# Moving the second half of a broadcast burst behind a score matmul in a one-core attention and feed-forward kernel

## What is computed

```
sc = scores.reshape(b, h, nb, WIN, nb, WIN)          # WIN = 128, nb = 8
sc = jnp.where(causal, sc, NEG_INF)
m = jnp.max(sc, axis=-1, keepdims=True)
e = jnp.where(causal, jnp.exp(sc - m), 0.0)
probs = e / jnp.where(denom == 0.0, 1.0, denom)       # denom = jnp.sum(e, axis=-1)
...
attn_probs = jax.nn.softmax(probs, axis=-1)
attn_out = jnp.einsum('bhqk,bhkd->bhqd', attn_probs, v)
```

## Time and profile before

| what | value |
|---|---|
| median of 3 runs | 2334.8 us (2330.03 to 2336.23) |
| the profiled execution | 2336.34 us, its span 2334.5 us |
| PE busy | 2192.1 us, 94% |
| DVE busy | 1732.6 us, 74% |
| ACT busy | 1510.2 us, 65% |
| POOL busy | 1166.3 us, 50% |
| mean granted TensorE clock | 0.989 of full |

### The profile page before, as it was taken

The page is one execution under the profiler, slowest core; times in us unless marked ns, Lnnn a source line. Parts: engine busy times, 40 slices in busy tenths (PEclk is TensorE's granted clock), DMA queues, the critical chain, the costliest instruction groups (busy, mean ns, idle before and its releaser), DMA issues.

```text
span 2334.5 us, 47167 instructions
## 1 busy us (share of the span) xinstructions
PE 2192.1 (94%) x19388; PEld 1241.9 (53%) x19388; DVE 1732.6 (74%) x2115; ACT 1510.2 (65%) x2101; POOL 1166.3 (50%) x1126
## 2 busy tenths in 40 slices
PE   6889889999999999999999999999999999989998
PEld 4444344465555555455554555545555555545567
DVE  6787888767787676876778776776877767787466
ACT  2477676766666667676776666766666666667741
POOL 3144134545665456744676257763576544443540
PEclk8999999999999999999999999999999999999999
DMA  5233122211122113111133202231022211101000
GB/s 181 72 107 98 49 55 82 85 48 39 50 68 85 53 35 91 60 51 53 35 91 96 59 9 59 67 109 49 14 65 78 84 35 46 40 16 31 6 28 25
DMA packets 114067, 140.26 MB, mean 60 GB/s; under 512 B 8648, under 2 KB 86760, under 8 KB 113856
## 3 DMA queue, kind: packets, MB, share of 16 engines
q1 hardware_dynamic: 113856, 137.24, 20.7%
HBM read 74.28 MB, written 58.74 MB: 57 GB/s over the span
## 4 chain that ended last, share of the span: by engine, by line
PE 77%; DVE 15%; ACT 3%; DMA 2%; issue 2%; POOL 2%; SPq 1%; ACTq 0%; POOLq 0%
PE pv L822 11%; PE sums L812 9%; PE ring L772 9%; PE score L742 9%; PE score L797 9%; PE sums L754 9%; DVE e L1178 6%; PE score L691 5%; DVE negmax L1156 4%; PE ring L851 4%; PE score L706 3%; PE ring L775 2%; PE score L800 2%; PE score L682 2%; ACT e L1052 2%
## 5 line engine op out<-in xcount | busy, mean ns | idle before, releaser
L1052 ACT ACTIVATE e<-score 128x512 f32<-128x512 f32 x1152 | 670.9, 595 | 400.7 <-PE score L800 220.6
L1178 DVE TENSOR_TENSOR e<-ring,e 128x1024 f32<-128x1024 f32 x576 | 677.5, 1217 | 282.6 <-PE ring L851 281.9
L1156 DVE TENSOR_REDUCE negmax<-ring 128x8 f32<-128x1024 f32 x576 | 679.5, 1220 | 140.5 <-PE ring L775 133.9
L1057 ACT ACTIVATE e<-e 128x2048 f32<-128x2048 f32 x288 | 548.6, 1905 | 3.7 <-DVE e L1178 3.6
L797 PE MATMUL score<-q_st,k_st 112*128 112x512 bf16 (+3 forms) x1536 | 459.7, 331 | 39.2 <-ACT e L1052 22.0
L772 PE MATMUL ring<-k_st,q_st 96*128 96x512 bf16 (+3 forms) x1664 | 389.1, 319 | 53.7 <-DVE e L1178 25.1
L1493 POOL TENSOR_SCALAR r_p<-r_b,ab 128x256 bf16<-128x256 f32 x96 | 88.6, 923 | 531.8 <-DVE r_b L1184 531.8
L822 PE MATMUL pv<-e,v 128*17 128x512 f32 (+3 forms) x3072 | 314.1, 496 | 1.1 <-DVE o_t L1196 1.1
L812 PE MATMUL sums<-e,d_ones 128*32 128x256 f32 x4608 | 304.6, 382 | 1.3
L1472 POOL TENSOR_TENSOR gT<-gT 128x512 f32<-128x512 f32 x112 | 115.9, 1040 | 333.5 <-ACT gT L1025 333.5
L797 PEld LDWEIGHTS score<-q_st,k_st 112*128 112x128 bf16 x1536 | 147.8, 97 | 228.9 <-issue 118.6
(11 more groups left out here) (149 smaller groups left out, 2518.3 us busy)
## 6 DMA issues: line engine op xcount, KB each, us to landing
q_st<-q_parts SPq DMA_DIRECT2D x31, 768.0 KB, 5.9
k_st<-k_parts SPq DMA_DIRECT2D x31, 768.0 KB, 8.6
q_parts<-qk_p SPq DMA_DIRECT2D x30, 384.0 KB, 2.6
k_parts<-qk_p SPq DMA_DIRECT2D x28, 384.0 KB, 2.5
x_in<-in_x SPq DMA_DIRECT2D x8, 1024.0 KB, 5.6
q_parts<-qk_p SPq DMA_DIRECT2D x30, 256.0 KB, 2.9
x_res<-in_x SPq DMA_DIRECT2D x30, 256.0 KB, 4.4
k_parts<-qk_p SPq DMA_DIRECT2D x28, 256.0 KB, 2.9
```

The lines of the kernel that those rows point to most:

```text
L1052: act.activation(e[:, n % ES, hh, :], score[SCORE_SLOT["st", n, hh][0]][:, :], ACT.Exp, scale=DK ** -0.5).then_inc(e1_done, 1)
L1057: act.activation(v, v, ACT.Exp).then_inc(e2_done, 1)
L1156: dve.tensor_reduce(negmax[:, at:at + NB // heads, hh:hh + heads].rearrange("p w h -> p h w"), slot[:, :].rearrange("p (h a n) -> p h a n" ...
L1178: dve.tensor_tensor(v, ring[no % 2][:, :].rearrange("p (i n) -> p i n", i=2), v, ALU.mult).then_inc(ring_free, 1)
```

## The change

The call for the second pair of heads moves from directly behind that for the first pair to directly behind the step's first score. Nothing is added or removed, and no other engine's order changes.

```
                 if 0 <= n - LAG_R < NUNIT:
                     one_over_sums(n - LAG_R, 0)
-                    one_over_sums(n - LAG_R, 1)
                 if piece_first(n) and p[0]:
...
                     if n < NUNIT:
                         scores(n, hh)
+                    if hh == 0 and 0 <= n - LAG_R < NUNIT:
+                        one_over_sums(n - LAG_R, 1)
                     if hh == 3 and 2 in at:
```

## The result

The changed kernel takes 2408.5 us (median of 4 runs, 2406.4 to 2412.7) against 2333.5 us for the kernel before (4 runs). The ratio is 1.0325, with a 95% interval of 1.0311 to 1.034: 75 us, 3.2% slower. The forecast was 2402 us, in a range of 2360 to 2447.

What follows compares the result with a forecast made beforehand. PE was taken to bound the kernel. 110 us of added PE work less 46 hidden gave 64, a second count 72; 67 was taken, giving 2402 us against the median of 2334.8, range 2360 to 2447.

Steps and rivals of the forecast that it cites:

- What bounds it: Whole kernel: PE bounds it, busy 94% of the span and 77% of the chain, against 15% for DVE.
- No gain at the ring: Pair 1's wait for the slot DVE's last reduce still reads: gain about 0, upper bound 31.8 us.
- The price of a half: Pair 1 alone behind score 0 costs PE 0.39 us per step, 110 us over 283 steps.
- some hundred us: Sum over all steps by the rule alone that a change of tiling mode drains TensorE, two more per step.
- What is hidden: PE's waits for DVE's multiply, a reduce and ACT absorb 46 us of the 110, between 24 and 68.
- Pair 1 late in the ninth steps: DVE stands 0.7 us in each of 31 ninth steps; costed at nothing, 22 us without cover.
- Pair 1 in time elsewhere: Ordinary steps: pair 1 ready at 1.19 us, before DVE finishes pair 0 at 1.62 us, so not late.
- Nothing is hidden: Rival: waits move behind PE's added work; 110 us, or 132 with ninth-step lateness, 2445 to 2467 us; chance 0.15.
- most is hidden: Rival: entry to the strips costs 0 and all waits absorb; 17 us slower, 2352 us; chance 0.09.
- faster: Rival: score 0 fills a real 31.8 us stall at the weight loads, half is free; 2309 us; chance 0.03.
- no difference: Rival: the half behind the score runs inside the whole-array matmul's stream; 6 us; chance 0.03.
- The check on ACT: Sign to look for after the change: ACT waits some 60 us more for scores.

Runs made afterwards that it cites:

- not_ninth: The move made in all steps but the ninth ones (252 steps), against the kernel before: 2404.4 us, ratio 1.0310.
- full_between: The kernel before with one extra 128-column matmul on the whole array between the two pairs, nothing moved: 2428.8 us, ratio 1.0417.
- pair1_twice: The kernel before with the four matmuls of pair 1 issued twice in a row: 2365.1 us, ratio 1.0151.
- strip_between: The kernel before with one extra 128-column matmul on one strip of 32 rows between the two pairs, nothing moved: 2338.7 us, ratio 1.0034.

## Why the prediction was right

- **What bounds it.** PE, as it said. The chain went to 84% PE.
- **No gain at the ring.** Right: the 31.8 us on the weight loads were no stall. The burst's matmuls had 0.3 us of idle time before and 0.0 after, and the loads' wait for the reduce stayed (29.8 us in 72). The reading of that row was off, though: 75 of the 76 waits stand at the burst's first load, which is pair 0's, while PE still works on the key sums. It says next to nothing of pair 1. Score 0 gained what was said, 0.01 to 0.02 us.
- **The price of a half, 0.32 + 0.09 - 0.02 = 0.39 us.** Right for the parts that were named: 0.32 to 0.33, and 0.15 against 0.06 at the entry. Some 57 us of the 110 are the two changes of mode (0.09 + 0.11, 283 times), and the rest is lost overlap; so the forecast's "some hundred us" from the rule on such changes alone doesn't hold. One term was missing, too. Where a piece with 4-byte operands stands behind the half, its first matmul costs 0.05 to 0.1 us more: that of line 742 takes 0.32 us to the next start behind a half, 0.27 behind a mask matmul, and 0.22 behind a score of 512 columns (medians). The timelines of PE in step 57, before and after:

```profile
458.92 0.39 PE L797 MATMUL score<-q_st,k_st 112*128 112x512 bf16 x1
459.14 1.89 PE L742 MATMUL score<-hT,w_fc 128*128 128x256 f32 x8
460.87 0.38 PE L797 MATMUL score<-q_st,k_st 112*128 112x512 bf16 x1
```

```profile
466.70 0.39 PE L851 MATMUL ring<-r_p,sel 32*128 32x256 bf16 x4
467.02 2.00 PE L742 MATMUL score<-hT,w_fc 128*128 128x256 f32 x8
468.86 0.38 PE L797 MATMUL score<-q_st,k_st 112*128 112x512 bf16 x1
```

  The piece takes 1.84 us instead of 1.73. In steps without a wait in either kernel the step grew by 0.41 us where a score stands behind the half (median of 8), by 0.45 with line 754 behind it (27) and by 0.50 with line 742 (56). Over 283 steps that is between 116 (all at 0.41) and 142 us (all at 0.50), not 110; PE's busy time rose by 116.8.
- **What is hidden, 46 us of 110.** Right in size, and partly by luck. PE's idle time fell by 40.5 us. But the waits that the forecast counted (for the multiply, for a reduce and for ACT at the scores) gave only 25.4 us of it (77.5 to 52.1). The waits for the multiply don't all vanish: 13.5 us in 46 stayed of 25.1 in 62, where the forecast let each of the 62 hide 0.39. The other 15 us come from waits that it didn't count. The largest is at the transposes, before and then after:

```profile
PE score L682 <- DVE x_in L1280: 9.8, 7, 1.5
```

```profile
PE score L682 <- DVE x_in L1281: 2.3, 7, 0.4
```

  So the ninth steps, which the sum treated like others, became shorter by 0.18 us on average though each paid for a half. not_ninth shows that the backlog which PE's delay clears is cleared across steps; a count of waits inside a step misses that. A second term was missing altogether, the clock: 12.6 us less at 1.2 GHz gave back up to 6 us. These and the missing 0.05 to 0.1 us of the price have opposite signs; that the sum came within 7 us of the result (2402 against 2408.5) owes something to that.
- **Pair 1 late in the ninth steps.** The total of 0.7 x 31 = 22 us of standing was met by luck: 22.7 us were measured, but as 1.0 us in each of 23 steps, DVE's alone. Costing it at nothing for PE was right: the ninth steps moved alone cost 5 us, less than 31 x 0.40 = 12.
- **Pair 1 in time elsewhere.** Right: no ordinary step has a gap between the multiplies.
- **The rivals.** "Nothing is hidden" (110) and "most is hidden" (17) both fell, "faster" and "no difference" with them: full_between and pair1_twice show that the half isn't free, and PE's idle time fell by 40.5 us, which is neither nothing nor most of 116.8.
- **The check on ACT.** ACT's idle time (span less busy) went from 824 to 888 us, 64 us more, near the 60 of the forecast, but not at the scores. There its waits grew from 381 to 394 us. The rest is at the pieces that share the score banks, most of it behind line 742, 125.3 and then 157.3 us:

```profile
ACT gT L1025 <- PE score L742: 125.3, 112, 2.6
```

```profile
ACT gT L1026 <- PE score L742: 157.3, 112, 2.6
```

## What to carry to other kernels

When small matmuls stand together and use different parts of the array, cost them as a block, not one by one: read the distance from the block's first start to the start behind it, and look for a place in the trace where a wait has torn it. Half of such a block alone may cost as much as the whole, and here each passage between strips and the whole array cost about 0.1 us. When a piece of work moves, compute when its reader wants it; inside that margin the move costs only its price; past it the loss here was three times that of the change (226 us against 75). And where the trace shows no wait, ask what covers it before moving the cover. When two kernels are compared by their step lengths, look first at which steps ran at the lower clock.

## What the runs showed of the hardware that was not expected

- The first matmul with 4-byte operands behind matmuls on row strips takes 0.1 us longer than its followers (0.32 against 0.22 us, line 742), beyond the 0.1 us of leaving the strips. Behind a mask matmul of 128 columns it takes 0.05 us longer, so it isn't the strips alone; the cause stays open.
- A matmul of 128 columns on one strip, between others on strips, lengthened the burst by 0.05 us (0.39 against 0.34); the same columns on the whole array lengthened it by 0.47 us (0.81 against 0.34).
- Matmuls on different strips need not start in program order: in strip_between the extra matmul is the fifth of the burst in the program and starts third, at 1225.62.
- Executions of one kernel differ mostly by the clock: those of the kernel before go from 2327.2 us at a mean granted clock of 0.994 of full to 2340.0 at 0.987.
